# Output transfers of a two-layer early-fusion transformer kernel: regrouped from one per sequence to one per token tile

## The reference, cut to what matters

```python
h = tokenizer(x)                          # patches -> 64 tokens, concatenated three times: (8, 192, 64)
h = concatenate([h, txt], axis=1)         # (8, 269, 64)
h = h + nystrom_attention(_layernorm(h))  # 8 heads, 128 landmarks, 6 pseudo-inverse steps, 33-tap conv
h = h + moe8_top2(_layernorm(h))          # 8 experts, gelu
h = h + distance_attention(_layernorm(h)) # 8 heads, scores = exp(-gamma * |q - k|^2)
h = h + ffn(_layernorm(h))                # below
return h                                  # (8, 269, 64) float32, 551 KB

def ffn(x):                               # the last stage, the one whose result is stored
    shared = relu(relu(x @ sW1 + sb1) @ sW2 + sb2) @ sW3 + sb3
    e = [relu(relu(x @ eW1[i] + eb1[i]) @ eW2[i] + eb2[i]) @ eW3[i] + eb3[i] for i in range(4)]
    gates = softmax(x @ gW + gb)          # top 2 of 4, softmax of the two
    return shared + sum(topw * chosen e)
```

## Time and profile before

| | us |
|---|---|
| median of three runs | 615.79 |
| lowest and highest of them | 615.77, 615.91 |
| the profiled execution's own time | 614.38 |
| its span, first to last recorded instruction | 612.5 |
| TensorE busy in the span | 560.1 (91%) |
| ScalarE busy | 374.4 (61%) |
| VectorE busy | 365.8 (60%) |
| GpSimd busy | 202.4 (33%) |

### The profile page before, as it was taken

One profiled execution on the slowest core, in us unless ns is written; L12 is line 12 of the kernel. 1 busy time (PEld: TensorE's weight loads), 2 busy tenths in 40 slices (PEclk: granted clock), 3 DMA queues, 4 the chain that ended last, 5 costly groups with the idle time before them and its releaser, 6 DMA issues. The chain is left out here.

```text
span 612.5 us, 26237 instructions
## 1 busy us (share of the span) xinstructions
PE 560.1 (91%) x11721; PEld 416.1 (68%) x11721; DVE 365.8 (60%) x737; ACT 374.4 (61%) x1005; POOL 202.4 (33%) x202
## 2 busy tenths in 40 slices
PE   8998997889888989898999899998999999998994
PEld 5686775777777878787786576665555555547672
DVE  2449457575757676767557433334677777773452
ACT  4567757685858585857542665553666666664731
POOL 5123356654555555555542003312011111111000
PEclk9999999999999999999999999999999999997898
DMA  8400000000000000000000000000000000000001
GB/s 282 164 2 2 3 4 3 4 4 4 3 5 3 5 4 5 3 6 4 4 2 3 1 3 2 2 2 1 2 3 2 2 2 2 3 2 1 1 12 28
DMA packets 5256, 9.03 MB, mean 15 GB/s; under 512 B 3608, under 2 KB 4120, under 8 KB 4760
## 3 DMA queue, kind: packets, MB, share of 16 engines
q1 hardware_dynamic: 4552, 7.29, 3.7%
q10 hardware_dynamic: 592, 0.07, 0.1%
HBM read 6.81 MB, written 0.55 MB: 12 GB/s over the span
## 5 line engine op out<-in xcount | busy, mean ns | idle before, releaser
L1430 POOL TENSOR_TENSOR STD<-STD,NN 128x512 f32<-128x512 f32 (+1 forms) x96 | 108.0, 1145 | 117.1 <-DVE NN L1597 104.1
L1597 DVE SCALAR_TENSOR_TENSOR NN<-ST,PS 128x512 f32<-128x512 f32 x96 | 64.0, 684 | 37.8 <-PE PS L954 37.4
L954 PE MATMUL PS<-ST 128*32 128x128 f32 x2304 | 76.3, 274 | 9.8 <-DVE ST L1603 5.7
L1603 DVE SCALAR_TENSOR_TENSOR ST<-PS,STD 128x512 f32<-128x512 f32 (+1 forms) x96 | 59.1, 624 | 42.8 <-POOL STD L1430 25.4
L954 PEld LDWEIGHTS PS<-ST 128*32 128x32 f32 x2304 | 60.8, 109 | 21.1 <-DVE ST L1603 12.7
L1276 ACT ACTIVATE STD<-ST 128x512 f32<-128x512 f32 (+1 forms) x96 | 53.3, 584 | 26.8 <-DVE ST L1603 25.8
L2196 DVE TENSOR_SCALAR GE<-PS,K 128x270 f32<-128x270 f32 x144 | 61.9, 489 | 8.8 <-PE PS L1901 8.0
L954 PE MATMUL PS<-NN 128*32 128x128 f32 (+1 forms) x2304 | 66.0, 261 | 0.5 <-DVE NN L1597 0.5
L954 PEld LDWEIGHTS PS<-NN 128*32 128x32 f32 x2304 | 55.6, 110 | 5.3 <-DVE NN L1597 2.5
L2026 ACT ACTIVATE GE<-PS,FB 128x540 f32<-128x540 f32 x64 | 42.0, 706 | 24.9 <-PE PS L1778 24.8
L2074 ACT ACTIVATE GE<-GE,NG 128x540 f32<-128x540 f32 (+1 forms) x80 | 51.5, 694 | 7.0 <-DVE GE L2196 7.0
(11 more groups left out here) (372 smaller groups left out, 1122.2 us busy)
## 6 DMA issues: line engine op xcount, KB each, us to landing
TP<-taps SPq DMA_DIRECT2D x1, 1204.0 KB, 16.2
MA<-mat SPq DMA_DIRECT2D x1, 1120.0 KB, 7.9
MF<-mat SPq DMA_DIRECT2D x1, 1024.0 KB, 13.0
WI<-wide SPq DMA_DIRECT2D x1, 934.0 KB, 9.5
CO<-const SPq DMA_DIRECT2D x1, 576.0 KB, 15.9
MQ<-mat SPq DMA_DIRECT2D x1, 512.0 KB, 16.6
out<-OS SPq DMA_DIRECT2D x8, 45.0 KB
XA<-xpatch SPq DMA_DIRECT2D x1, 256.0 KB, 2.8
```

The costliest lines, as they stand in the source:

```text
L954: last = nc.tensor.matmul(PS[32 * g:32 * g + 32, PINV + q, k * SW + c0:(k + 1) * SW], x[:, h, 32 * m:32 * m + 32], x[:, h, c0:SW], start=T ...
L1430: nc.gpsimd.tensor_tensor(TD[:, 4 * q:4 * q + 4, c0:SW], SA[:, 4 * q:4 * q + 4, c0:SW], NN[:, 4 * q:4 * q + 4, c0:SW], ALU.subtract).then_ ...
L1597: v.scalar_tensor_tensor(out=NN[:, own, :], in0=ST[:, b % 2, own, :], scalar=N_S, in1=heads4(PS[:, PINV + q, 0:4 * SW]), op0=ALU.mult, op1 ...
L1603: v.scalar_tensor_tensor(out=ST[:, b % 2, own, c0:SW], in0=heads4(PS[:, PINV + q, 0:4 * SW])[:, :, c0:SW], scalar=S_M, in1=TD[:, own, c0:S ...
```

## The change

The helper `put` begins one transfer of rows `lo` to `hi` of token tile `t`, for both sequences of pair `p`. A pair's four transfers are now: tile 0 (90 partitions x 2 rows), tile 1 (90 x 2), tile 2 without its last token (88 x 2) and that last token (1 x 2). Of the last pair, SyncE begins the first and the third, ScalarE the second and the fourth, behind its last copy. There are still sixteen transfers and 256 counts.

```diff
+        def put(eng, p, t, lo=0, hi=TT):
+
+            eng.dma_start(out[2 * p:2 * p + 2, t * TT + lo:t * TT + hi, :].rearrange("b p d -> p b d"), OS[lo:hi, p, :, t, :]
+                          ).then_inc(sem("g_put"), 16)
+
+        REST = N - 2 * TT
+
         with nc.Block() as block:
             @block.sync
             def _(sp):
                 for p in range(BP):
                     need(sp, emptied("flip", p))
-                    for o in range(2):
-                        sp.dma_start(out[2 * p + o:2 * p + o + 1, 0:2 * TT, :].rearrange("b (t p) d -> p (b t) d", p=TT),
-                                     OS[:, p, o, 0:2, :]).then_inc(sem("g_put"), 16)
-                        sp.dma_start(out[2 * p + o:2 * p + o + 1, 2 * TT:N, :].rearrange("b p d -> p (b d)"),
-                                     OS[0:N - 2 * TT, p, o, 2, :]).then_inc(sem("g_put"), 16)
-                sp.wait_ge(sem("g_put"), 32 * B)
+                    put(sp, p, 0)
+                    if p < BP - 1:
+                        put(sp, p, 1)
+                    put(sp, p, 2, 0, REST - 1)
+                    if p < BP - 1:
+                        put(sp, p, 2, REST - 1, REST)
+                sp.wait_ge(sem("g_put"), 64 * BP)
...
                 flip(2)
                 flip(3)
+                need(act, emptied("flip", BP - 1))
+                put(act, BP - 1, 1)
+                put(act, BP - 1, 2, REST - 1, REST)
```

## The result

| | before | changed |
|---|---|---|
| median, us | 616.14 (16 runs, 613.64 to 624.18) | 612.80 (16 runs, 608.61 to 615.09) |
| ratio | | 0.9935 (0.9913 to 0.9957) |
| profiled execution, us | 614.38 | 614.28 |
| its span, us | 612.5 | 612.4 |
| end of ScalarE's last copy, us | 605.18 | 608.45 |

What follows compares the result with a forecast made beforehand. Compute bounds the kernel up to 605.18 us, then one slow DMA engine's stores set the end. Issues, packets, landing and barrier end the span at 609.30 instead of 612.5, so 615.79 - 3.2 = 612.6 us; range 611.5 to 614.2.

Steps and rivals of the forecast that it cites:

- The lane: Final stores: one DMA engine working off all rows of 89-partition transfers sets the end; its load falls from 5.81 to 1.27 us.
- the 1.46 us issue: SyncE's longest issue among the final stores at 606.73, the others taking 0.28 to 0.61; explained by a full DMA engine list.
- The issues, added up: SyncE's six issues for pairs 2 and 3 become the limit, running from 604.10 to 607.16 us.
- Behind the last issue: After SyncE's last issue: 0.49 us to first packet, 0.35 to last, 0.33 to the waiting SyncE, 0.97 of barrier.
- ScalarE's share: ScalarE's two issues behind the last copy cost nothing; on SyncE alone they would add 0.93 us.
- The cover: Margin by which ScalarE's last packets end before SyncE's at 608.0: 0.6 us or more.
- Turns in issuing: Rival: SyncE's and ScalarE's issues exclude each other in the final stores; gain only 1.9 to 2.5 us; chance 0.13.
- The long issue: Rival: the number of transfers under way lengthens one of pair 3's issues by 0.9 us; gain 2.3 us; chance 0.09.
- Division over the sequences: Rival: each transfer is divided by its two sequences instead of its tokens, making the kernel 1.4 us slower; chance 0.03.
- A late landing: Rival: final completions come late for another reason, such as ScalarE's idle queue; 614.6 to 616.4 us; chance 0.05.
- A sign that failed: Compute up to ScalarE's last copy should stay unchanged; if its end moves over 0.5 us, the sum doesn't cover it.
- The time: Whole kernel: forecast median 612.6 us, from 615.79 less 3.2, with chance 0.70.

Runs made afterwards that it cites:

- 88 rows: The kernel before, with only the last token tile stored without its last token (88 partitions instead of 89): tail from last copy to span's end 4.10 us, against 7.32.
- Changed again: The changed kernel itself, with every issue on a source line of its own: tail 3.98 us, ratio 0.9940 to the kernel before.
- GpSimd part: Changed kernel, but GpSimd begins pair 2's 88 tokens and all last tokens in one transfer, ScalarE only the last pair's 88 tokens: tail 3.45 us, ratio 0.9925.
- Tiles of 96: Changed kernel, but output turned and stored in tiles of 96, 96 and 77 tokens, ScalarE beginning only the last pair's tile 1: tail 3.15 us, ratio 0.9952.
- Tokens once: Changed kernel, but the last tokens of all eight sequences go in one transfer begun by ScalarE after its last copy, none on SyncE: tail 3.50 us.

## Why the prediction was right

- *The lane.* Right in kind and place. One engine took all rows of an 89-partition transfer, the 1.46 us issue was its echo, and both went: 88 rows in the kernel before give 4.10 us of tail. That is 3.2 of the 3.4 us by which the changed kernel's tail is shorter.
- *The issues, added up.* From SyncE's first issue of pair 2 to the end of its sixth 3.06 us were forecast (604.10 to 607.16), 2.76 measured (607.37 to 610.13). Two terms were mis-sized and partly cancelled. A large transfer behind another takes 0.37 to 0.44 us, not 0.55, because the 0.56 and 0.61 that I took were already lengthened by the lane; the single token takes 0.58 to 0.60, not 0.28.
- *Behind the last issue.* 0.49 + 0.35 us forecast to the last packet, 0.96 measured (610.13 to 611.09); then 0.34 to the waiting SyncE and 0.97 of barrier, as forecast. The tail was to be 609.30 - 605.18 = 4.12 us and is 3.95, so the gain in it is 3.37 us for 3.2.
- *ScalarE's share.* 0.93 forecast, 0.86 measured. Its issues were mis-sized, though: with 0.62 and 0.73 us they end 1.42 us behind the copy, later than the 0.75 to 1.31 of the prediction. The cover held, but smaller: SyncE's last ends at 1.68, and ScalarE's last packet (610.59) is 0.5 us before SyncE's, where 0.6 or more was forecast.
- *Rivals.* Turns in issuing: SyncE's issues are the same, within 0.06 us, when it issues alone. The lock that the Trainium skill describes ("Perfetto Trace Analysis", DMA Instruction, HWDGE) is not seen to lengthen them in these runs. The long issue: none over 0.6 on SyncE from pair 2 on. Division over the sequences: 15 and 11 engines by the packet counts. A late landing: 1.3 us of final wait for 1.2 forecast.
- *A sign that failed.* The end of the last copy was to move by no more than 0.5 us; it moved by 3.27, and by the prediction's own words the sum then doesn't cover it. But it moves as much between two profiles of the changed kernel's stores, from 608.45 to 611.52 in Changed again, and in the pair of before and changed the granted clock differs where the phases' lengths do. The sign supposed a steadiness that the compute doesn't have. That the placement of the code adds nothing wasn't shown apart.
- *The time.* 612.6 us forecast from a median before of 615.79, 612.80 measured beside one of 616.14. That they meet within 0.2 us is in part luck, since either kernel's executions spread over 6 us or more; the gain is what was forecast. The ratio's 4.0 us exceed the tail's 3.37, inside the interval from 2.7 to 5.4, and nothing beyond the tail has to be explained by the stores.

The misses were in the experiments. With the full lane kept, I took its packets alone for its length, and both runs that kept it under the new issuing came out 0.8 to 0.9 us above. GpSimd part came out 0.35 above its forecast; 88 rows, Tiles of 96 and Tokens once came out 0.1 to 0.2 below theirs.

## What to carry to other kernels

Look at the partition count of every transfer near the end of a kernel: in these runs 89 partitions put all rows on one DMA engine at 18 GB/s and 86 on two at 36, where 88 had 11 engines and 90 had 15; an even plateau behind the last issue is the mark. Take one row away and judge by the stretch from the last computation to the end, since the whole time varies by more than the gain. Better than cutting off a single row, whose issue takes 0.6 us here, is to choose the tile sizes so that each count divides by a large number up to 16 (for 269: 96, 96 and 77, which divide by 16, 16 and 11).

## What the runs showed of the hardware

Transfers from a single partition were long to begin: two rows took 0.58 to 0.72 us on SyncE and 0.72 on ScalarE, eight rows 0.79 on ScalarE. The forms of 154 to 192 rows over 11 to 16 engines took 0.32 to 0.45 on SyncE. Few rows as such aren't dear: 3 partitions x 2 rows took 0.29 us on ScalarE (and 0.57 on SyncE, there behind 86 x 2). Forms that go to one or two engines were short to begin themselves, 0.27 to 0.33 us for 89 partitions and for 86. But the issue behind one on the same queue was long: 0.53 to 0.56 us for a 45 KB transfer behind one of 89 rows, against 0.34 to 0.36 behind one of 88. An issue's length thus follows neither bytes nor rows; why wasn't settled.

ScalarE's issues are not of one length: 0.61 to 0.66 us for 90 x 2 rows in five runs, 0.36 for 96 x 2 in the one that has it.
